# Attention loop on one Trainium2 core: ScalarE copies every second half of the turned probabilities and issues the operand loads

## The reference, cut to what matters

```python
scores = jnp.einsum('bhqd,bhkd->bhqk', Q, K) * scale
c2p = jnp.take_along_axis(c2p, rel_pos[None, None, :, :], axis=-1)
p2c = jnp.swapaxes(jnp.take_along_axis(p2c, p2c_pos[None, None, :, :], axis=-1), -1, -2)
probs = jax.nn.softmax(scores + c2p + p2c, axis=-1)
ctx = jnp.einsum('bhqk,bhkd->bhqd', probs, V)
```

## Time and profile before

| | us |
|---|---|
| median of three runs | 9684.97 |
| the profiled execution's own time | 9684.03 |
| its span | 9682.3 |
| of it the attention loop, first to last exponential | 566.1 to 3750.4 |

### The profile page before, as it was taken

The page is one execution under the profiler, slowest core; times in us unless marked ns, Lnnn a source line. Parts: engine busy times, 40 slices in busy tenths (PEclk is TensorE's granted clock), DMA queues, the critical chain, the costliest instruction groups (busy, mean ns, idle before and its releaser), DMA issues. The chain is left out here.

```text
span 9682.3 us, 173958 instructions
## 1 busy us (share of the span) xinstructions
PE 8268.4 (85%) x48396; PEld 4738.3 (49%) x48396; DVE 8401.1 (87%) x13204; ACT 5602.5 (58%) x9153; POOL 4998.8 (52%) x4685
## 2 busy tenths in 40 slices
PE   5679999999999997599688888887688888888599
PEld 2356667666666665366233333333233333333366
DVE  4668888888888886799599999999599999999799
ACT  2257777777777774233466666665466656555233
POOL 0000000000000000388599999999599999999487
PEclk7789999999999998799899999999899999999799
DMA  6789888888888887211112222111122222221111
GB/s 191 252 266 284 278 283 282 282 282 282 282 280 282 280 284 224 71 42 42 72 66 78 80 80 80 72 55 75 63 78 86 89 89 89 89 75 65 46 42 41
DMA packets 1174163, 1447.35 MB, mean 149 GB/s; under 512 B 83658, under 2 KB 1053914, under 8 KB 1140992
## 3 DMA queue, kind: packets, MB, share of 16 engines
q1 hardware_dynamic: 1173824, 1444.18, 45.4%
HBM read 880.81 MB, written 564.60 MB: 149 GB/s over the span
## 5 line engine op out<-in xcount | busy, mean ns | idle before, releaser
L1964 POOL TENSOR_TENSOR mb_bx<-mb_dtu,mb_bc 128x512 f32<-128x512 f32 x2048 | 2665.2, 1325 | 7.7 <-DVE mb_hs L2064 7.4
L2207 PE MATMUL mb_y_ps<-mb_g,ident 128*128 128x512 f32 x4096 | 2189.0, 641 | 467.9 <-DVE mb_g L2024 238.1
L2251 ACT ACTIVATE mb_dA<-mb_dt,mb_a_neg 128x512 f32<-128x512 f32 x2048 | 1403.3, 689 | 1616.2 <-DVE mb_hs L2064 1080.0
L1400 POOL MEMSET f_magic<- 128x1 f32 x2 | 0.2, 99 | 3617.7 <-POOLq L127 3617.7
L2207 PEld LDWEIGHTS mb_y_ps<-mb_g,ident 128*128 128x128 f32 x4096 | 763.6, 199 | 1646.1 <-issue 726.1
L1011 ACT ACTIVATE at_tab<-at_e_ps 128x384 f32<-128x384 f32 x2064 | 1015.1, 492 | 774.9 <-PE at_e_ps L928 773.5
L1065 DVE TENSOR_REDUCE at_nmax<-at_s_ps 128x1 f32<-128x1024 f32 x1025 | 1255.4, 1225 | 35.2
L944 PE MATMUL at_pT_ps<-ident,at_probs 128*128 128x128 f32 x8192 | 1117.7, 279 | 102.5 <-ACT at_probs L1016 81.9
L1016 ACT ACTIVATE at_probs<-at_s_ps,at_nmax 128x1024 f32<-128x1024 f32 x1025 | 1142.9, 1115 | 60.4 <-DVE at_nmax L1065 39.2
L944 PEld LDWEIGHTS at_pT_ps<-ident,at_probs 128*128 128x128 f32 x8192 | 894.3, 141 | 413.2 <-ACT at_probs L1016 384.9
L2024 DVE TENSOR_TENSOR mb_g<-mb_hs,mb_bc 128x512 f32<-128x512 f32 x1472 | 996.1, 677 | 33.8 <-PE mb_y_ps L2207 32.4
(11 more groups left out here) (236 smaller groups left out, 14151.9 us busy)
## 6 DMA issues: line engine op xcount, KB each, us to landing
at_tables<-at_tab SPq DMA_DIRECT2D x1032, 384.0 KB, 3.9
at_skew<-at_tables SPq DMA_DIRECT2D x1030, 256.0 KB, 3.1
mb_bc<-mb_bc_rows SPq DMA_DIRECT2D x256, 1024.0 KB, 6.4
at_skew<-at_tables SPq DMA_DIRECT2D x773, 128.0 KB, 3.5
at_opnd<-at_q_st SPq DMA_DIRECT2D x130, 210.0 KB, 4.4
at_opnd<-at_kl_st SPq DMA_DIRECT2D x130, 210.0 KB, 4.7
at_opnd<-at_kr_st SPq DMA_DIRECT2D x130, 210.0 KB, 4.7
at_q_st<-st_parts SPq DMA_DIRECT2D x96, 256.0 KB, 3.2
```

What stands on the lines that cost most here:

```text
L1964: pool.tensor_tensor(bx[:, s % RINGS, :], dtu[:, c, :], bc[:, 0, n, :], ALU.mult).then_inc(s_bx, 1)
L2207: nc.tensor.matmul(y_ps[:, c % 2, :], ident[:, :], g[:, s1 % RINGS, :], start=False, stop=(n == STATE - 1)).then_inc(s_y, 1)
L2251: nc.scalar.activation(dA[:, s % DA_RING, :], dt[:, c, :], ACT.Exp, scale=a_neg[:, c, n:n + 1]).then_inc(s_dA, 1)
```

## The change

On ACT, `keep_second` runs in every iteration, not only in odd ones; DVE's copy L1073 is gone, and one semaphore (`second_half_kept`) takes the place of the two. In iteration 6, the three operand loads of head `n+2` are issued by ACT, between `exps` and `keep_second`, instead of by SP, which also loses its wait for the scores there. The loads of the first two heads, ahead of the loop, stay on SP.

```diff
@@ SP, head(h)
-                    if i == TT - 2:
-                        ge(sp, s_S, n * TT + TT)
-                        load_opnd(n + 2, u)
                     store_tables(n + 1, 1 - u, i)
@@ PE, turn and context
-                    elif i % 2 == 1:
-                        ge(pe, s_p1v, n * HALF + (i + 1) // 2)
                     else:
-                        ge(pe, s_p1a, n * HALF + i // 2)
+                        ge(pe, s_p1, m)
...
-                if i0 % 2 == 0:
-                    ge(pe, s_p1v, h.n * HALF + i0 // 2 + 1)
-                else:
-                    ge(pe, s_p1a, h.n * HALF + i0 // 2 + 1)
+                ge(pe, s_p1, h.n * TT + i0 + 1)
@@ ACT
-                nc.scalar.activation(probsT[:, i % 2, HC:T], pT_ps[:, 1, 0:HC], ACT.Copy).then_inc(s_p1a, 1)
+                nc.scalar.activation(probsT[:, i % 2, HC:T], pT_ps[:, 1, 0:HC], ACT.Copy).then_inc(s_p1, 1)
...
+            def load_opnd(n, u):
+
+                ge(act, s_E, (n - 1) * NE)
+                for k, st in enumerate((q_st, kl_st, kr_st)):
+                    act.dma_start(opnd[:, u, k, :],
+                                  st[bass.ds(n, 1), :, :].rearrange("a r t -> (a r) t")).then_inc(s_op[k][u], 16)
...
                         exps(m + 1, (i + 1) % TT)
-                        if i % 2 == 1:
-                            keep_second(m, i, n)
+                        if i == TT - 2:
+                            load_opnd(n + 2, u)
+                        keep_second(m, i, n)
                         if i % GROUP == 0 and not (isinstance(m, int) and m == 0):
@@ DVE, keep_turned
-                if i % 2 == 0:
-                    ge(dve, s_T, m * 2 + 2)
-                    nc.vector.tensor_copy(probsT[:, i % 2, HC:T], pT_ps[:, 1, 0:HC]).then_inc(s_p1v, 1)
```

More of the change, by code:

```diff
@@ L763, in attention_loop @@
     LANES = P // VW
-    HALF = TT // 2
     SUM = BANK - GROUP * VW
@@ L799, in attention_loop @@
         s_T, s_pv, s_cT = sem("turned"), sem("context"), sem("context_kept")
-        s_p0, s_p1v, s_p1a = sem("first_half_kept"), sem("second_half_kept_even"), sem("second_half_kept_odd")
+        s_p0, s_p1 = sem("first_half_kept"), sem("second_half_kept")
         s_pick, s_sel, s_share, s_out = sem("pick"), sem("context_summed"), sem("share"), sem("out")
```

## The result

The changed kernel takes 9880.96 us (median of 4 runs, 9869.99 to 9889.83) against 9686.01 (median of 4, 9678.15 to 9688.5): a ratio of 1.0202, 95% interval 1.0189 to 1.0214. It is slower by 195 us. The forecast was 9950 in a range of 9800 to 10100, with 0.90 on slower.

What follows compares the result with a forecast made beforehand. The prediction took a ring of waits between PE and ACT in the attention loop as the bound; 0.05 + 0.96 + 0.82 + 0.25 = 2.08 us a head, x128 = 266, on 9684 gave 9950 us, range 9800 to 10100.

Steps and rivals of the forecast that it cites:

- DVE's relief: Attention loop, even iterations: dropping DVE's copy gains 0, as DVE's maximum is not what comes last; at most 0.3 us a head.
- The ring through the table copy: Plain loop iterations: exponential, transposes, second table product, ACT's table copy, next exponential set the pace, once round in 2.85 us.
- The copies in iterations 0 and 4: ACT, beside the context copy: no room left, so each added copy delays the rest by 0.48 us; 0.96 a head.
- The copy in iteration 2: ACT, no context copy there: the added copy slightly delays the table product and last transposes; 0.05 us a head.
- The issues: ACT, iteration 6: three load issues hold its queue, so tile 6's copy and the last transposes wait; 0.82 us a head.
- The landing: Load of `q_st`, leaving ACT 1.57 us later than SP, lands late for its table product; 0.25 us a head.

Runs made afterwards that it cites:

- e4: The kernel before without the even iterations' second-half copy on any engine, so DVE is relieved and ACT gets nothing more: 9696.76 us, ratio 1.0006.
- e1: The changed kernel with the three operand loads back on SP, so only the copies differ from the kernel before: 9809.54 us, ratio 1.0122.
- e2: The kernel before with only the three operand loads moved to ACT, DVE still copying in even iterations: 9699.91 us, ratio 1.0008.
- e5: The changed kernel with the three loads issued behind the second-half copy instead of ahead of it, in the same iteration: 9837.98 us, ratio 1.0148.
- e7: The changed kernel with only the third load on ACT and the other two back on SP: 9816.4 us, ratio 1.0125.

## Why the prediction was right

The direction, the place and the mechanism of the cost held: second-half copies that push back the context copy and the table copy, and issues that hold up a copy. The sizes were too large, 2.08 us a head against 1.53 (26.41 - 24.88; x128 = 196 us). One reading was wrong without harm to the sum. Term by term:

1. **DVE's relief, taken as 0.** e4 gives it alone: 1.0006, 0. The figure held, but the reason given for it did not, and here the forecast had luck. I compared the reported ends of the maximum and of the table copy and found the copy later. But an exponential starts before the table copy's reported end: where that copy is the last to come, it starts 0.39 behind the copy's start (2506.02 to 2506.41). In the two iterations that I read, the distance is 0.58 and 0.45, and the exponential follows the maximum's end by 0.12 and 0.11 (2509.38 to 2509.50, 2512.31 to 2512.42). Over all heads the exponentials of tiles 2 to 7 behave so, with 0.12 behind the maximum and 0.42 to 0.74 behind the table copy's start; only tile 0 has 0.39. So the maximum came last in at least six of eight iterations, and the 39.2 us of listed waits hid it. Its relief is worth nothing since the maximum waits for scores in its turn (e4). The ring through the table copy, as I told it, set the pace only ahead of tile 0 in the kernel before; in the changed kernel it does so for tiles 0, 2, 4 and 6 (0.39 behind the table copy), and the columns that end there, 7, 1, 3 and 5, have most of the cost.
2. **The copies in iterations 0 and 4, taken as 0.96.** Columns 1, 2, 5 and 6 grow by 0.36 + 0.08 + 0.31 + 0.13 = 0.88, in e1 too. That is 0.44 a place and not 0.48: the exponential that followed had a few hundredths of slack, as it had been waiting for the maximum.
3. **The copy in iteration 2, taken as 0.05.** Columns 3 and 4: -0.03 + 0.08 = 0.05.
4. **The issues, taken as 0.82.** Column 7 grows by 0.63, of which 0.05 is the copy alone (e1). The place was right: the copy late, the transposes split, PE waiting. The size was off since the copy could start 1.47 behind the first issue (2503.76 to 2505.23), not the 1.63 of SP's row, and the table product came 2.77 behind the exponential's start, not 2.92. SP's figure had in it a last issue of 0.56.
5. **The landing, taken as 0.25.** Gone: column 0 is 3.04 against 3.06. This is the term that failed. Part of it was a misreading: the 4.6 of the earlier trace rows is the median of all three loads, and the first alone has 4.4, which would have left 0.05 of the 0.25 (line below). The rest went with an earlier landing: `q_st` landed 3.6 behind its issue on ACT, not 4.4 as on SP: 2503.76 + 3.6 = 2507.4, ahead of its table product at 2508.01. e2 shows 3.5 for the same load with DVE and ACT copying as before. That agrees with the rule that the Trainium skill gives (DMA: Bandwidth & Descriptors, Queues, rings and completion order) of a ring for each issuing engine, served in turn. No run tests that rule by itself. I had given it a sentence and not the sum.

```profile
at_opnd<-at_q_st SPq DMA_DIRECT2D x128, 210.0 KB, 4.4
```

What the sum did not say, and e2 does: the issues' cost is not theirs. Alone it is 14 us of loop, ahead of the copy of tile 6 it is 73, and behind that copy 25 (e5).

## What to carry to other kernels

Before moving work to the engine that is less busy, find which of its instructions stands behind the new one in its queue and who waits for that: here an engine with a quarter of its time free had none to spare in two of eight iterations, and the same copies cost 0.95 us a head there and about 0.25 once one other copy stood elsewhere. In this kernel a transfer issued from ACT cost what its issue delayed beyond the instruction that was already running: nothing for one, 0.08 us a head for two, 0.58 for three. And to see which of two inputs came last, measure from one instruction's start to the next; a reported end can lie behind the point at which the next one starts (ACT's table copy: 0.49 reported, 0.39 to the next start), and a short wait then stands in no list.

## What was not expected of the hardware

The first of the three loads of 210 KB, `q_st`, landed a median of 3.5 us behind its issue from ACT, beside 4.4 and 4.3 from SP in kernels that are otherwise the same (e2 against before; e5 against e1, 1000 to 3500 us). The second gained as well, 3.8 against 4.7 and 3.7 against 4.5. The third did not always: 4.0 against 4.7 in e2, but 4.7 against 4.6 in e5. Which part of it is the ring and which the moment of the issue was not separated: with only the third load moved to ACT (e7), `q_st` on SP landed in 3.8.
